# Feed-forward of a decoder layer: halves of W1 made once in the attention loop, high halves written by ScalarE from PSUM, output statistics spread over the tile

## The reference, cut to what matters

```python
def _layer_norm(x, gamma, beta, eps=1e-12):
    mu = jnp.mean(x, axis=-1, keepdims=True)
    var = jnp.mean(jnp.square(x - mu), axis=-1, keepdims=True)
    return (x - mu) * jax.lax.rsqrt(var + eps) * gamma + beta

def _L0_ffn_ref(hidden_states, W_router, W1, b1, Wo, bo, ln_gamma, ln_beta):
    x = hidden_states.reshape(-1, H)                     # H = 256, I = 1024, E = 4
    expert_idx = jnp.argmax(x @ W_router, axis=-1)
    h = jnp.einsum('th,ehi->tei', x, W1) + b1
    h = jax.nn.gelu(h, approximate=False)
    onehot = jax.nn.one_hot(expert_idx, E, dtype=x.dtype)
    intermediate = jnp.einsum('te,tei->ti', onehot, h)
    y = intermediate @ Wo + bo + x
    return _layer_norm(y, ln_gamma, ln_beta).reshape(B, S, H)

x = x + _L0_attn_ref(_layernorm(x), L0_attn_W, L0_attn_b)
x = x + _L0_xattn_ref(_layernorm(x), ctx_1024, L0_xattn_Wq, L0_xattn_Wkv, L0_xattn_Wc)
x = x + _L0_ffn_ref(_layernorm(x), L0_ffn_W_router, L0_ffn_W1, ...)
```

## Time and profile before

| | |
|---|---|
| time, median of 3 runs | 4378.67 us (4378.36 to 4382.7) |
| profiled execution, span | 4384.2 us (the page gives no other time of this execution) |
| busy share of the span | PE 80%, DVE 69%, ACT 36%, POOL 33% |
| attention loop | about 0 to 3246 us |
| feed-forward, first product of `widen` to last of `narrow` | 3278.6 to 4368.7 us, 35 tiles |
| VectorE busy in 3400 to 4150 us | 741.73 of 750 us |

### The profile page before, as it was taken

The page is one execution under the profiler, slowest core; times in us unless marked ns, Lnnn a source line. Parts: engine busy times, 40 slices in busy tenths (PEclk is TensorE's granted clock), DMA queues, the critical chain, the costliest instruction groups (busy, mean ns, idle before and its releaser), DMA issues.

```text
span 4384.2 us, 86021 instructions
## 1 busy us (share of the span) xinstructions
PE 3487.1 (80%) x26632; PEld 2620.2 (60%) x26632; DVE 3030.9 (69%) x7302; ACT 1595.7 (36%) x2976; POOL 1468.2 (33%) x1785
## 2 busy tenths in 40 slices
PE   5788778887788777887788778887748888888887
PEld 3555555555555555555555555555537777777777
DVE  3666656665666656665666656665649999999997
ACT  2444444444444444444444444444412222222221
POOL 3222222222222222222222222222225656565655
PEclk7888888888888888888888889888858889888888
DMA  6455554455455554555455554555321212212120
GB/s 126 78 92 94 96 89 84 89 99 93 85 90 95 94 89 84 93 96 95 82 90 95 94 89 89 92 95 93 61 76 63 68 65 67 67 64 67 65 67 32
DMA packets 341784, 366.25 MB, mean 84 GB/s; under 512 B 58456, under 2 KB 319071, under 8 KB 341728
## 3 DMA queue, kind: packets, MB, share of 16 engines
q1 hardware_dynamic: 324768, 330.85, 41.8%
q0 software_dynamic: 12864, 33.64, 2.1%
q10 hardware_dynamic: 4096, 1.06, 0.1%
HBM read 251.56 MB, written 113.32 MB: 83 GB/s over the span
## 4 chain that ended last, share of the span: by engine, by line
PE 29%; DVE 24%; DMA 21%; issue 12%; ACT 4%; POOL 4%; SPq 3%; DVEq 1%; POOLq 0%; ACTq 0%
DMA parts_qc<-cq_parts 12%; DMA QC<-parts_qc 8%; DVE hT_high L1405 8%; PE psum L660 4%; PE psum L724 4%; SPq L457 3%; PE psum L565 3%; PE psum L638 3%; PE psum L647 2%; PE psum L611 2%; PE psum L559 2%; PE psum L751 2%; POOL cq_parts L1535 2%; PE psum L662 2%; PE psum L644 2%
## 5 line engine op out<-in xcount | busy, mean ns | idle before, releaser
L1131 DVE TENSOR_REDUCE cnegmax<-psum 128x4 f32<-128x480 f32 x512 | 324.3, 654 | 662.1 <-PE psum L724 661.9
L964 ACT ACTIVATE PA<-psum 128x512 f32<-128x512 f32 x512 | 294.9, 596 | 881.3 <-PE psum L647 879.9
L724 PE MATMUL psum<-KCx,QC 97*128 97x120 bf16 x2048 | 243.7, 256 | 332.7 <-DMA QC<-parts_qc 331.0
L1058 ACT ACTIVATE hT<-psum,b_sb 128x512 f32<-128x512 f32 x280 | 193.2, 690 | 848.1 <-PE psum L884 848.1
L900 PE MATMUL psum<-wo_high,hT_low 128*128 128x256 f32 x1120 | 385.4, 344 | 131.1 <-DVE hT_low L1408 69.0
L1124 DVE TENSOR_REDUCE negmax<-psum 128x2 f32<-128x512 f32 x512 | 340.9, 687 | 154.1 <-PE psum L614 153.8
L724 PEld LDWEIGHTS psum<-KCx,QC 97*128 97x128 bf16 x2048 | 190.4, 119 | 404.3 <-issue 347.3
L638 PE MATMUL psum<-QP,KP 98*128 98x256 bf16 x1024 | 240.8, 327 | 164.7 <-DMA QP<-mxT 164.7
L1405 DVE CAST hT_high<-hT 128x512 fp32r<-128x512 f32 x280 | 359.7, 1295 | 3.9 <-ACT hT L1058 3.7
L900 PEld LDWEIGHTS psum<-wo_high,hT_low 128*128 128x128 f32 x1120 | 252.7, 226 | 177.1 <-DVE hT_low L1408 95.9
L900 PE MATMUL psum<-wo_low,hT_high 128*128 128x256 f32 x1120 | 354.9, 317 | 0.0
(11 more groups left out here) (211 smaller groups left out, 8867.8 us busy)
## 6 DMA issues: line engine op xcount, KB each, us to landing
QP<-parts_q SPq DMA_DIRECT2D x384, 128.0 KB, 4.5
KP<-parts_k SPq DMA_DIRECT2D x384, 128.0 KB, 7.8
QC<-parts_qc SPq DMA_DIRECT2D x384, 128.0 KB, 4.6
w_sb<-in_w SPq DMA_DIRECT2D x35, 1024.0 KB, 4.8
parts_q<-q_parts SPq DMA_DIRECT2D x64, 384.0 KB, 2.6
parts_k<-k_parts SPq DMA_DIRECT2D x64, 384.0 KB, 2.6
parts_qc<-cq_parts SPq DMA_DIRECT2D x64, 384.0 KB, 8.4
fx<-rows_dram SPq DMA_DIRECT2D x35, 514.0 KB, 3.8
```

The source lines that it names most:

```text
L724: last = pe.matmul(psum[:, bank, j * M:(j + 1) * M], QC[0:KS, par, 4 * g + j, t * P:(t + 1) * P], KCx[0:KS, par, 0:M], start=True, stop=True)
L964: act.activation(dst, psum[:, ST_BANKS[n % 2], :], ACT.Exp, scale=D ** -0.5).then_inc(exp_done.sem, 1)
L1131: dve.tensor_reduce(cnegmax[:, t, 4 * g:4 * g + 4], psum[:, S_BANKS[n % 2], 0:4 * M].rearrange("p (h k) -> p h k", h=4), AX_X, ALU.max).th ...
```

## The change

It has four parts.

1. **W1.** In each round of the attention loop SyncE loads a sixty-fourth of all four experts' W1 (128 partitions x 128 float32, 64 KB), GpSimd makes its two halves (a cast and a subtraction, behind `k_parts` and ahead of `cq_parts`), and SyncE stores both to DRAM in the next round. In the feed-forward SyncE loads the ready halves of the expert (2 x 1 MB) in place of W1, and VectorE's and GpSimd's work on them is gone.
2. **High halves.** ScalarE writes `fzT_high` straight from PSUM in place of `fzT`, and applies the gelu twice to each PSUM block, once into `hT_high` and once into `hT`. VectorE's casts are gone; it makes `fzT_low` from PSUM, and all eight `hT_low`.
3. **Order on VectorE.** The output statistics, their aggregation and the centering of tile k - 2 stand between the eight `hT_low` of tile k - 1. The input statistics of tile k + 1 stand behind the finish of tile k - 2.
4. **Wo.** Its split moves from ahead of the first tile to behind the first `fzT_low`.

```diff
@@ SyncE, attention loop
+            def load_w1_piece(b, par):
+                if begun(b - 2):
+                    sp.wait_ge(w1_piece_split.sem, w1_piece_split.value(b - 2))
+                sp.dma_start(w1_in[:, par], w1_piece(w1, b)).then_inc(w1_piece_in[par].sem, 16)
+            def store_w1_piece(b, par):
+                sp.wait_ge(w1_piece_split.sem, w1_piece_split.value(b))
+                sp.dma_start(w1_piece(w1_high_dram, b), w1_up[:, par].bitcast(F32)).then_inc(w1_piece_out[par].sem, 16)
+                sp.dma_start(w1_piece(w1_low_dram, b), w1_rest[:, par].bitcast(F32)).then_inc(w1_piece_out[par].sem, 16)
...
@@ SyncE, load_weights
-                sp.dma_start(w1_sb[:, par], w1[bass.ds(expert, 1)].rearrange("o (c p) i -> p (o c) i", p=P)).then_inc(w1_loaded[par].sem, 16)
+                sp.dma_start(w1_high[:, par].bitcast(F32), w1_high_dram[bass.ds(expert, 1)].rearrange("o (c p) i -> p (o c) i", p=P)).then_inc(w1_loaded[par].sem, 16)
+                sp.dma_start(w1_low[:, par].bitcast(F32), w1_low_dram[bass.ds(expert, 1)].rearrange("o (c p) i -> p (o c) i", p=P)).then_inc(w1_loaded[par].sem, 16)
...
@@ TensorE: turn_tile waits for z_low_made in place of fzT_copied, widen for w1_loaded
-                pe.wait_ge(w1_low_made.sem, w1_low_made.value(b))
+                pe.wait_ge(w1_loaded[q].sem, w1_loaded[q].value(b // 2))
...
@@ ScalarE
+                        act.activation(hT_high[:, m, :], psum[:, m % 4, :], ACT.Gelu, bias=b1_sb[:, q, m:m + 1])
                         act.activation(hT[:, m, :], psum[:, m % 4, :], ACT.Gelu, bias=b1_sb[:, q, m:m + 1]).then_inc(gelu_done.sem, 1)
...
-                        copy(fzT[:, kc, :], psum[:, 6 + kc, :]).then_inc(fzT_copied.sem, 1)
+                        copy(fzT_high[:, kc, :], psum[:, 6 + kc, :]).then_inc(z_high_made.sem, 1)
...
@@ VectorE, tile_body
-                if tile_runs(k, 0):
-                    split_w1(k, par)
-                if tile_runs(k, 1):
-                    split_h(k - 1)
+                for m in range(MI):
+                    if tile_runs(k, 1):
+                        split_h(k - 1, m)
+                    if m in (0, 2) and tile_runs(k, 2):
+                        out_statistics(k - 2, (m, m + 1))
+                    if m == 3 and tile_runs(k, 2):
+                        out_aggregate(k - 2)
+                    if m in (4, 6) and tile_runs(k, 2):
+                        center(k - 2, (m - 4, m - 3))
...
@@ GpSimd, attention loop
+            def split_w1_piece(b, par):
+                if begun(b - 2):
+                    pool.wait_ge(w1_piece_out[par].sem, w1_piece_out[par].value((b - 2) // 2))
+                pool.wait_ge(w1_piece_in[par].sem, w1_piece_in[par].value(b // 2))
+                pool.tensor_copy(w1_up[:, par], w1_in[:, par]).then_inc(w1_piece_split.sem, 1)
+                pool.wait_ge(w1_piece_split.sem, w1_piece_split.value(b, 1))
+                pool.tensor_tensor(w1_rest[:, par], w1_in[:, par], w1_up[:, par], ALU.subtract).then_inc(w1_piece_split.sem, 1)
```

More of the change, by code:

```diff
@@ L35 @@
 OUT_LN_EPS = 1e-12
-H_LOW_POOL = (5, 7)
-H_LOW_DVE = tuple(m for m in range(MI) if m not in H_LOW_POOL)
 Q_PARTS = (0, 0, 0, 1, 1, 2)
@@ L463, in body @@
                     load_x(i + 2, par)
+                    load_w1_piece(i, par)
+                if runs(i, 1):
+                    store_w1_piece(i - 1, 1 - par)
                 if runs(i, 1):
@@ L507, in _ @@
                 sp.wait_ge(rows_sent[par].sem, rows_sent[par].value(B // 2 - 1))
+            for par in range(2):
+                sp.wait_ge(w1_piece_out[par].sem, w1_piece_out[par].value(B // 2 - 1))
             sp.wait_ge(plan_step, PLAN_STEPS)
@@ L1372, in _, with split_wo @@
             dve.wait_ge(weights_in, 16 * N_WEIGHT_LOADS)
[L1373 to L1377, removed]
+            def split_wo():
+                for n in range(2):
+                    dve.tensor_copy(wo_high[:, 4 * n:4 * n + 4, :], wo_sb[:, 4 * n:4 * n + 4, :]).then_inc(wo_split, 1)
+                for n in range(2):
+                    dve.wait_ge(wo_split, n + 1)
+                    dve.tensor_tensor(wo_low[:, 4 * n:4 * n + 4, :], wo_sb[:, 4 * n:4 * n + 4, :], wo_high[:, 4 * n:4 * n + 4, :], ALU.subtract).then_inc(wo_split, 1)
             def tile_statistics(k, par):
@@ L1417, in add_z, with out_statistics, out_aggregate @@
                     dve.tensor_tensor(ysum[:, 2 * half:2 * half + 2, :], psum[:, 4 + half, :].rearrange("p (j c) -> p j c", j=2), zb[:, par, 2 * half:2 * half + 2, :], ALU.add).then_inc(ysum_made.sem, 1)
-            def out_statistics(b):
-                for j in range(TS):
+            def out_statistics(b, rows):
+                for j in rows:
                     dve.wait_ge(ysum_made.sem, ysum_made.value(b, j // 2 + 1))
                     dve.bn_stats(ostats[:, j, :], ysum[:, j, :]).then_inc(oln_step.sem, 1)
+            def out_aggregate(b):
                 for j in range(TS):
@@ L1426, in out_statistics, with center, finish @@
                     dve.bn_aggr(omv[:, j, :], ostats[:, j, :]).then_inc(oln_step.sem, 1)
-            def finish(b, par):
-                for j in range(TS):
+            def center(b, rows):
+                for j in rows:
                     dve.wait_ge(oln_step.sem, oln_step.value(b, TS + j + 1))
                     dve.scalar_tensor_tensor(ysum[:, j, :], ysum[:, j, :], omv[:, j, 0:1], gamma_sb[:], ALU.subtract, ALU.mult).then_inc(oln_step.sem, 1)
+            def finish(b, par):
                 dve.wait_ge(oln_rstd.sem, oln_rstd.value(b))
@@ L1589, in tile_body @@
                 if tile_runs(k, 0):
-                    for kc in range(KC):
-                        pool.wait_ge(w1_high_made.sem, w1_high_made.value(k, kc + 1))
-                        pool.sem_inc(passed_pool, 1)
-                        pool.tensor_tensor(w1_low[:, par, kc, :], w1_sb[:, par, kc, :], w1_high[:, par, kc, :], ALU.subtract).then_inc(w1_low_made.sem, 1)
                     if begun(k - 2):
@@ L1599, in tile_body @@
                     pool.tensor_tensor(zb[:, par], fz[:], bo_sb[:].unsqueeze(1).broadcast_to([P, TS, C]), ALU.add).then_inc(zb_made.sem, 1)
-                if tile_runs(k, 1):
-                    for m in H_LOW_POOL:
-                        pool.wait_ge(h_high_made.sem, h_high_made.value(k - 1, m + 1))
-                        pool.sem_inc(passed_pool, 1)
-                        pool.tensor_tensor(hT_low[:, m, :], hT[:, m, :], hT_high[:, m, :], ALU.subtract).then_inc(h_low_pool.sem, 1)
                 if tile_runs(k, 2):
```

65 lines of the change are left out of this document (31 added, 34 removed).

## The result

The change makes the kernel faster: 4104.15 us (4101.68 to 4109.93) beside 4378.51 us (4376.9 to 4382.7) for the kernel before, a ratio of 0.9365 with a 95% interval of 0.9349 to 0.9381.

What follows compares the result with a forecast made beforehand. VectorE, shut out of SBUF by GpSimd's operations, was taken to bound the feed-forward. 4384.2 - 266 (feed-forward) - 3 (start) + 1 (attention loop) = 4116 us profiled, 5.5 us over the median, so 4111 us; range 4094 to 4150.

Steps and rivals of the forecast that it cites:

- VectorE's lock was the bound of the stage, and TensorE becomes it: Feed-forward: GpSimd's SBUF operations shut VectorE out, 31.1 us a tile; after the change TensorE's 23.2 us bounds it.
- VectorE's 20.6 us: Feed-forward: VectorE's time per tile after the change, 18.2 us of work plus up to 2.41 us of lock by zb.
- 18.2 us: Feed-forward: VectorE's busy time per tile left from 30.8 us once the casts go and two hT_low are added.
- rival 1: Feed-forward: VectorE or ScalarE stays the bound; 4154 us at 1.55 us per ScalarE block, or 4178 at VectorE's 25.4; chance 0.10.
- ScalarE's 1.18 us a block: Feed-forward widening: two gelus at 0.59 us per block, hidden behind the 1.36 us TensorE takes to make it.
- A tile at 23.2 + 0.3: Feed-forward: TensorE's own 23.2 us per tile plus 0.3 us lost to stalls, bounds 0 and 1.3.
- The stalls of 10.5 us: Feed-forward: TensorE's assumed loss of 0.3 us in each of 35 tiles.
- The start, -3: Ahead of first widening: 6 us less wait for the split rows, partly offset by their later load; 3 us net gain.
- The attention loop, +1: Attention loop: W1's pieces fit idle time, steady cost 0 (bounds 0 and 2.3 us per round), 1 us once.
- W1's halves hidden, Wo's split free, the end unchanged: Feed-forward: 2 MB of halves land in about 10 us, due over 30 later; Wo's split and the end cost nothing.
- Rivals 2 and 3: Attention loop: pieces lengthen the path, 4130 to 4258 us, chance 0.13; or land too late, 4495 at 22 us, chance 0.04.
- part 3 as neutral: Feed-forward, VectorE: the spread statistics were counted as the same instructions in other places, with nothing saved.

Runs made afterwards that it cites:

- act_only: Kernel before with only ScalarE writing the high halves and VectorE making all hT_low; W1 still split in each tile: 4223.67 us, ratio 0.9606.
- w1_only: Kernel before with only W1's halves made in the attention loop and loaded; activation casts stay on VectorE: 4191.36 us, ratio 0.9537.
- lock_read2: Changed kernel plus two GpSimd sums per tile behind zb that read and write SBUF, result unused: 4226.85 us, ratio 0.9633.
- lock_write2: Changed kernel plus five GpSimd memsets of 128x1024 per tile behind zb, which only write: 4117.7 us, ratio 0.9375.
- rows_first2: Changed kernel with the first tile's rows loaded ahead of the first expert's halves of W1: 4114.23 us, one run.
- pieces_only: Kernel before plus W1's pieces loaded, split and stored in the attention loop, result unused: 4393.34 us, ratio 0.9995.
- kp_late2: Changed kernel with the six packing transfers of KP issued behind the store and packing of QC in the attention loop: 3798.25 us, ratio 0.8651.

## Why the prediction was right

The forecast was 4111 us, the time 4104.15. Step by step:

- **VectorE's lock was the bound of the stage, and TensorE becomes it.** Right. TensorE 600.00 of 600 at 1.00. Casts and lock each had a share: `act_only` takes ten casts away and keeps the lock, at 26.44 us a tile; `w1_only` takes W1's lock (4.78 us) and its two casts (1.3) away and saves 200.6 / 35 = 5.7 us; `lock_read2` gives 4.05 us of lock back to the kernel after and loses 3.2 us a tile; `lock_write2` gives back as much work without it and loses nothing.
- **VectorE's 20.6 us.** 518.42 / 600 x 23.30 = 20.1. In it are some 2.5 us of lock by `zb` and 2.1 by `xb`. The prediction names `zb`'s alone, but its 18.2 us held `xb`'s already, since a locked operation counts as busy. So rival 1's 25.4 us counts both twice, and its 4178 us was too dear.
- **ScalarE's 1.18 us a block.** Right. The float32r gelu takes 0.69 us like its neighbour, and pairs start 0.59 us apart (3582.02, 3582.61). Rival 1's bound of 1.55 had no ground.
- **A tile at 23.2 + 0.3.** Measured 23.30. The pair was put to end at 12.4 us and the last `hT_low` at 13.6 to 14.5, due at 14.2; it ends at 13.55. The stalls of 10.5 us in the sum didn't come. The stage is 817.77 for 824.4. This term, 6.6 us, and the start, 1.65, are about the 8 us by which the predicted span of 4116 was too long. That nothing else moved the total is partly luck: the attention loop, put at +1, varies by more than this from one execution to the next.
- **The start, -3.** Measured -4.65. The wait for the split rows shrank from 7.57 to 1.50, the 6 us of the prediction, but the rows' load was only 1.4 us later, not 3. `rows_first2` shows that 3.9 us still lay in the order of these loads.
- **The attention loop, +1.** +0.6 between two executions, which is within what they vary by; `pieces_only` bounds the cost at 2.2 us. The piece takes GpSimd 0.9 us from `k_parts` on and SyncE its idle time.
- **W1's halves hidden, Wo's split free, the end unchanged.** Right: no wait of TensorE for either, and 15.5 us behind the last sum in both kernels.
- **Rivals 2 and 3** had a way through SyncE's queue. The queue does set the round, as `kp_late2` shows, but at the twelve packings ahead of `parts_qc`, not where the pieces stand.

The prediction took part 3 as neutral and didn't ask when it would cost. That it can, shown only in a kernel with more lock, was the one surprise of sign.

## What to carry to other kernels

Work that depends only on weights and is redone in each tile can be moved to an earlier stage with idle engines, if each of its steps falls into an idle stretch of its own engine and of the DMA queue. When two engines share a lock, price the move by the operations that are slowed and by the clock that their waits cost TensorE, not by the busy time of the engine that slows them; and don't add up gains that each end at the same next bound. In a queue, put the transfer on which the round waits ahead of those that have time.

## What the runs showed of the hardware that was not expected

- An engine that is shut out stays so over several operations that follow each other back to back, on either side. A subtraction of VectorE takes 5.13 us in `lock_read2`, over `zb` and the sum behind it, and ends 0.57 us behind that sum, where GpSimd leaves a gap of 0.18 us: it did its whole work after the lock. GpSimd's `zb` takes 5.69 us in the first tile of the kernel after, over six subtractions.
- `fz`, a VectorE operation with one large input in SBUF, is shut out too: 3.50 us for four beside `xb`, 1.38 us without it.
- The order of recorded starts doesn't always tell which engine is shut out: 0.26 us ahead of `zb` VectorE won (kernel after, 3284.50), 0.29 us ahead it lost where `zb` stood directly behind a DMA issue (`lock_read2`, 3574.18).
- GpSimd's memsets, 4.8 us a tile, slow VectorE's subtractions by nothing (0.67 us each beside them).
- A 384 KB store took 8.45 us behind twelve packings of 128 KB and 2.52 us in `kp_late2`, where only the six of QP are ahead of it and their issue ended 3.7 us before.
